# Cross attention in a fused decoder: value products in other pieces, the square turn in two instructions, and TensorE's order in a tile

## What is computed

```python
kv_rope = kv_c * cos[None] + _rotate_half(kv_c) * sin[None]
q_r = jnp.einsum('bshq,hqr->bhsr', q_big, W_qr)
k_r = jnp.einsum('bld,hdr->bhlr', kv_rope, W_kr)
scores = jnp.einsum('bhsr,bhlr->bhsl', q_r, k_r)
attn = jax.nn.softmax(scores, axis=-1)
ctx_c = jnp.einsum('bhsl,bld->bhsd', attn, kv_rope)
ctx_lat = jnp.einsum('bhsd,hkd->bshk', ctx_c, w_kc_kv)
out = ctx_lat.reshape(b, s, H * K) @ Wo.T
```

## Time and profile before

| | |
|---|---|
| time, median of 3 runs | 3219.04 us (3218.99 to 3221.29) |
| profiled execution, its own time | 3230.32 us |
| its span | 3228.3 us |
| granted TensorE clock, mean | 0.952 |
| busy, TensorE | 2933.8 us (91%) |
| busy, VectorE | 1862.5 us (58%) |
| busy, ScalarE | 1242.3 us (38%) |
| busy, POOL | 872.7 us (27%) |

### The profile page before, as it was taken

One profiled execution on the slowest core, in us unless ns is written; L12 is line 12 of the kernel. 1 busy time (PEld: TensorE's weight loads), 2 busy tenths in 40 slices (PEclk: granted clock), 3 DMA queues, 4 the chain that ended last, 5 costly groups with the idle time before them and its releaser, 6 DMA issues. The chain is left out here.

```text
span 3228.3 us, 47818 instructions
## 1 busy us (share of the span) xinstructions
PE 2933.8 (91%) x17993; PEld 1709.2 (53%) x17997; DVE 1862.5 (58%) x3321; ACT 1242.3 (38%) x1997; POOL 872.7 (27%) x743
## 2 busy tenths in 40 slices
PE   4889998988999989899998989989899998677999
PEld 3655555554455453355555557753355555446444
DVE  6557887733232257788885233347788885655222
ACT  3446656521111142455554122222455653424221
POOL 4324555410316024433333000004333333201000
PEclk8899999988999989999999999999999999888999
DMA  1146677622122212277776010012277775001111
GB/s 32 48 120 161 166 174 166 145 66 95 63 91 78 88 28 81 62 165 158 158 165 162 13 42 25 25 43 74 65 170 155 166 168 125 15 12 23 39 39 33
DMA packets 221440, 299.21 MB, mean 93 GB/s; under 512 B 127178, under 2 KB 149052, under 8 KB 218764
## 3 DMA queue, kind: packets, MB, share of 16 engines
q1 hardware_dynamic: 220348, 294.39, 37.4%
q10 hardware_dynamic: 864, 1.77, 0.2%
HBM read 120.52 MB, written 21.38 MB: 44 GB/s over the span
## 5 line engine op out<-in xcount | busy, mean ns | idle before, releaser
L1786 ACT ACTIVATE l1x_shared<-l1x_shared,l1x_a_low 128x1500 f32<-128x1500 f32 x112 | 173.1, 1546 | 159.8 <-DVE l1x_shared L1740 156.9
L1786 ACT ACTIVATE l2x_shared<-l2x_shared,l2x_a_low 128x1500 f32<-128x1500 f32 x112 | 173.1, 1546 | 158.4 <-DVE l2x_shared L1740 156.8
L1786 ACT ACTIVATE l0x_shared<-l0x_shared,l0x_a_low 128x1500 f32<-128x1500 f32 x112 | 173.2, 1546 | 139.5 <-DVE l0x_shared L1740 138.1
L1656 PE MATMUL l0x_a_S_ps<-l0x_kt,l0x_a_q 64*128 64x366 f32 (+1 forms) x896 | 176.4, 507 | 4.4 <-issue 2.5
L1656 PE MATMUL l1x_a_S_ps<-l1x_kt,l1x_a_q 64*128 64x366 f32 (+1 forms) x896 | 175.9, 506 | 2.2 <-DVE l1x_shared L1740 1.9
L1656 PE MATMUL l2x_a_S_ps<-l2x_kt,l2x_a_q 64*128 64x366 f32 (+1 forms) x896 | 174.9, 505 | 2.0 <-DVE l2x_shared L1740 1.6
L2026 DVE TENSOR_TENSOR l0f_times_up<-l0f_gate,l0f_U 128x448 f32<-128x448 f32 x64 | 39.7, 621 | 236.9 <-PE l0f_U L1944 236.9
L1995 ACT ACTIVATE l0f_gate<-l0f_G 128x448 f32<-128x448 f32 x72 | 39.1, 543 | 310.7 <-PE l0f_G L1939 310.7
L1353 POOL TENSOR_TENSOR l2x_q_straight<-l2x_q_straight,l2x_q_crossed 128x448 f32<-128x448 f32 x48 | 54.5, 1135 | 340.5 <-DVE l2x_q_crossed L1344 340.5
L1740 DVE TENSOR_SCALAR_CACHE_REDUCE l0x_shared<-l0x_a_S_ps 128x768 f32<-128x768 f32 x112 | 107.3, 958 | 66.0 <-PE l0x_a_S_ps L1656 57.4
L1740 DVE TENSOR_SCALAR_CACHE_REDUCE l2x_shared<-l2x_a_S_ps 128x768 f32<-128x768 f32 x112 | 107.3, 958 | 53.7 <-PE l2x_a_S_ps L1656 50.2
(11 more groups left out here) (672 smaller groups left out, 6474.2 us busy)
## 6 DMA issues: line engine op xcount, KB each, us to landing
l0x_space<-normed SPq DMA_DIRECT2D x192, 128.0 KB
l1x_space<-normed SPq DMA_DIRECT2D x192, 128.0 KB
l2x_space<-normed SPq DMA_DIRECT2D x192, 128.0 KB
l0x_space<-l0x_a_blocks SPq DMA_DIRECT2D x186, 96.0 KB, 2.8
l1x_space<-l1x_a_blocks SPq DMA_DIRECT2D x186, 96.0 KB, 3.6
...
```

Source lines behind the costliest of these rows:

```text
L1656: last = pe.matmul(S_ps[:, 2 * pair + rows_, 0:w], q[lane, b % 2, k * 128:(k + 1) * 128], kt[lane, b % 2, pair * W1:pair * W1 + w], start= ...
L1786: act.activation(p[:, n % 2], p[:, n % 2], ACT.Exp, bias=low[:, n % 2, 1:2], scale=-1.0, accum_out=den[:, b % 2, k:k + 1]).then_inc(exp_re ...
```

## The change

1. The value products are cut into other pieces: `PIECES` has eight entries in place of seven, with 1, 3, 3, 3, 2 + 1, 4, 4 and 3 slots. The last piece of a batch stands in tile 5 of the next batch (entry 12), where it was in tile 4 (entry 11).
2. TensorE's order in a tile is transposes, values, scores; it was transposes, scores, values.
3. The square turn is two instructions: the six inner squares of each row, then the two outer ones. The first half of `negate`, which overwrites only what the inner squares read, waits for `inner_blocked`, the second half for `outer_blocked`. Whoever waited for `blocked` waits for both.
4. ScalarE copies `C_ps` out one tile later, at tiles 3 and 6.

```diff
--- before.py
+++ after.py
@@ -1430,7 +1430,8 @@
     T, N = QT_TILES, QT_TILES * B
     FIRST, COUNT = (0, 4), (4, 3)
     W1, W2, JB = 3 * KD, KD + 2 * KP, NB * 32
-    PIECES = {5: (0, 0, 2), 6: (0, 2, 4), 7: (0, 4, 8), 8: (0, 8, 12), 9: (1, 0, 4), 10: (1, 4, 8), 11: (1, 8, 12)}
+    PIECES = {5: [(0, 0, 1)], 6: [(0, 1, 4)], 7: [(0, 4, 7)], 8: [(0, 7, 10)], 9: [(0, 10, 12), (1, 0, 1)],
+              10: [(1, 1, 5)], 11: [(1, 5, 9)], 12: [(1, 9, 12)]}
     TURNED_AT = (0, KP, LK - 2 * KP, LK - KP)
     SLOTS = (8, 10, 9, 11, 6, 0, 2, 4, 1, 3, 5, 7)
     ctx, kt, v, nv = ahead.ctx, ahead.kt, ahead.v, ahead.nv
@@ -1467,7 +1468,8 @@
         exp_ready = st.sem(name + "exp_ready")
         turned = st.sem(name + "turned")
         pt_kept = st.sem(name + "pt_kept")
-        blocked = st.sem(name + "blocked")
+        inner_blocked = st.sem(name + "inner_blocked")
+        outer_blocked = st.sem(name + "outer_blocked")
         moved = [[st.sem(f"{name}moved{g}{j}") for j in range(2)] for g in range(2)]
         kept_own = st.sem(name + "kept_own")
         rden_ready = st.sem(name + "rden_ready")
@@ -1493,7 +1495,8 @@
 
         def move(eng, b, g, lanes):
 
-            eng.wait_ge(blocked, T * b + FIRST[g] + COUNT[g])
+            eng.wait_ge(inner_blocked, T * b + FIRST[g] + COUNT[g])
+            eng.wait_ge(outer_blocked, T * b + FIRST[g] + COUNT[g])
             if b > 0:
                 eng.wait_ge(valued, 2 * (b - 1) + g + 1)
             for l in lanes:
@@ -1580,7 +1583,8 @@
 
                 def own(b, g):
 
-                    pool.wait_ge(blocked, T * b + FIRST[g] + COUNT[g])
+                    pool.wait_ge(inner_blocked, T * b + FIRST[g] + COUNT[g])
+                    pool.wait_ge(outer_blocked, T * b + FIRST[g] + COUNT[g])
                     if b > 0:
                         pool.wait_ge(valued, 2 * (b - 1) + g + 1)
                     if ctx is not None:
@@ -1713,16 +1717,17 @@
                 for n in range(N):
                     b, k = n // T, n % T
                     turn(n)
+                    for piece in PIECES.get(k + T, []) if b > 0 else []:
+                        values(b - 1, *piece)
+                    for piece in PIECES.get(k, []):
+                        values(b, *piece)
                     if n + 2 < N:
                         scores(n + 2)
-                    if k > 4:
-                        values(b, *PIECES[k])
-                    elif b > 0:
-                        values(b - 1, *PIECES[k + T])
                     if ctx is not None and k == 4 and b + 1 < B:
                         turn_keys(b + 1)
-                for k in range(T, T + 5):
-                    values(B - 1, *PIECES[k])
+                for k in range(T, T + 6):
+                    for piece in PIECES[k]:
+                        values(B - 1, *piece)
 
             @block.vector
             def _(dve):
@@ -1733,9 +1738,11 @@
                         dve.wait_ge(scored, 2 * n + pair + 1)
                         if pair == 0 and n > 1:
                             dve.wait_ge(turned, n - 1)
-                            dve.wait_ge(blocked, n - 1)
+                            dve.wait_ge(inner_blocked, n - 1)
                         if pair == 1:
                             dve.wait_ge(passed, 2 * n + 1)
+                            if n > 1:
+                                dve.wait_ge(outer_blocked, n - 1)
                         start = n % 2 * LK + at
                         dve.tensor_scalar(ahead.shared[:, start:start + 2 * apart].rearrange("q (a k) -> q a k", a=2)[:, :, 0:w],
                                           S_ps[:, 2 * pair:2 * pair + 2, 0:w],
@@ -1750,8 +1757,10 @@
                     if b > 0 and k == FIRST[g]:
                         dve.wait_ge(moved[g][(b - 1) % 2], 192 * ((b - 1) // 2 + 1))
                         dve.wait_ge(kept_own, 8 * (b - 1) + 4 * g + 4)
-                    dve.transpose(blocks[g][:, :, k - FIRST[g]].rearrange("q l j b -> q j l b"),
-                                  p[:, n % 2, 2 * KP:LK - 2 * KP].rearrange("q (j l b) -> q j l b", j=NB, l=4)).then_inc(blocked, 1)
+                    to = blocks[g][:, :, k - FIRST[g]].rearrange("q l j b -> q j l b")
+                    squares = p[:, n % 2, 2 * KP:LK - 2 * KP].rearrange("q (j l b) -> q j l b", j=NB, l=4)
+                    dve.transpose(to[:, 1:NB - 1], squares[:, 1:NB - 1]).then_inc(inner_blocked, 1)
+                    dve.transpose(to[:, 0:NB:NB - 1], squares[:, 0:NB:NB - 1]).then_inc(outer_blocked, 1)
 
                 def invert(b):
 
@@ -1820,9 +1829,9 @@
                 exp(1)
                 for n in range(N):
                     b, k = n // T, n % T
-                    if k == 2 and b > 0:
+                    if k == 3 and b > 0:
                         keep_contexts(b - 1, 0)
-                    if k == 5 and b > 0:
+                    if k == 6 and b > 0:
                         keep_contexts(b - 1, 1)
                     keep(n)
                     if ctx is not None and k == 4 and b + 1 < B:
```

## The result

The changed kernel takes 3316.37 us (median of 4 runs, 3309.56 to 3323.13), the kernel before 3219.01 us (median of 4, 3214.14 to 3221.29): 1.0304 times as long, with an interval of 1.028 to 1.0329. The profiled execution of the changed kernel took 3309.56 us with a span of 3306.6 us, against 3230.32 and 3228.3: +79.2 us, where the prediction's sum was +79 on that same execution.

What follows compares the result with a forecast made beforehand. The attention loop was taken as bound by TensorE, with a loop through POOL nearly closed in layer 0. Terms 59 + 16 + 4 = +79 us on the profiled 3230.32 gave 3309, put at 3298 us on the median; range 3245 to 3340.

Steps and rivals of the forecast that it cites:

- The offset to the median: Whole kernel: the profiled execution lies 0.35% above the median, so the sum of 3309 us became 3298 us.
- The loop through POOL in layer 0: Last values, POOL's rope and copies, next batch's block products: 32.5 us per batch against 27.97, +59 us.
- the slow clock: Layer 0, after TensorE's wait for POOL: 1.6 us added per batch; +59 us with it, +38 without.
- Which part closes the loop: Layer 0: last values behind the keys' turn and first block product ahead of scores make 30.89 us against 27.97.
- The late moves of layers 1 and 2: Block moves start 1.45 us later and are wanted sooner; nine late batches wait 1.8 us longer, +16 us.
- The split turn: VectorE's square turn: 0.00 to 0.12 us more, a 0.15 us wait given back, hidden behind TensorE; taken as zero.
- Spread pieces and seams: TensorE's tiles: pieces stay 10.15 us, undisturbed batches 24.78 us, seams as before; no gain, seam bound 17 us.
- The ends of the layers: Last tile of the three layers: scores, exponential, turn and moves come one piece later, 3 x 1.45 = +4 us.
- both tight loops snap: Rival, slower still: exponential loop or VectorE's second turn paces most tiles, 34 to 67 us more; chance 0.10.
- the change hardly acts: Rival: POOL's rope was not waiting for the values, layer 0 keeps its period, +4 to +20 us; chance 0.07.
- it is faster: Rival: steadier DMA pace ends late moves of layers 1 and 2, 38 us saved, 3181 us; chance 0.07.

Runs made afterwards that it cites:

- The extra transposes: Changed kernel with 24 unused TensorE transposes per batch laid into its wait for POOL in tile 0 of layer 0: 3312.9 us, 1.0222.
- the inverses in longer runs: Inverse sums laid out in DRAM as (q, k), not (k, q): kernel before 3174.93 us, 0.9853; changed kernel 3258.99 us, 1.0125.
- the copies first: Changed kernel with POOL's own copies of group 0 ahead of its rope: 3259.07 us, 1.0136.

## Why the prediction was right, point by point

3298 us was forecast and 3316.37 measured, within 3245 to 3340, and slower. On the profiled execution the sum was off by less than 1 us, and that is luck: layer 0's loop grew by 75 us (59 forecast), those of layers 1 and 2 by 8 (16 forecast), and the rest shrank by 5 (4 more forecast). The offset to the median missed as well: the changed kernel's median lies 7 us above its profiled execution, where the kernel before lay 11 below.

- **The loop through POOL in layer 0** was the cause, as put: 13 waits of 4.0 us (4.1 forecast), POOL's part 10.20 us (10.18), and the loss goes when the rope stands behind the copies. The term was too small: 33.98 us per batch, not 32.5, +78 us over 13 batches, not +59. What was mis-sized is the slow clock. From last values to last values the loop takes 35.6 us and 32.4 us in turn (one 33.05), where the sum had 31.40 + 1.6 and 30.38 + 1.6. From the first block product of tile 0 to the end of the tile, 2.91 us at full clock, it takes 5.56 us in six long turns of the loop and 4.55 in the six short ones (4.22 in the odd one): 2.1 us lost on average, and not 1.6. In six of the seven batches with the longer keys' turn the last three slots, in tile 5, lose another 1.0 us or more (3.0 us from the transposes' start to their end, and not 1.8), because the clock falls again behind the keys' turn. The sum took the clock as one loss per batch, from a row of layer 1, where there is no keys' turn; with the last values in tile 5 that second fall came to lie within the loop. The two falls together cost 2.6 us per batch where 1.6 was put, and this 1.0 is about two thirds of what the term was short by. Another 0.3 us per batch is a term that the sum left out, for the most part TensorE's wait for ScalarE in front of the keys' turn. The extra transposes bear out the part in tile 0; the one in tile 5 was not taken away by itself.
- **Which part closes the loop** was put partly wrong. The text named two things, the last values behind the keys' turn and the first block product ahead of the scores. The pieces alone give the whole wait (52.7 us) in the old order, and the order alone gives next to none (1.4 us). The order moves both ends of the loop by the same scores, and cancels; only the tile counts. What the order adds in layer 0 is the 0.3 us in front of the keys' turn (that wait is in the run with the order alone, 13 times, and in the run with the pieces alone only once), and some slow clock: 33.98 us per batch against 33.27 with the pieces alone.
- **The late moves of layers 1 and 2** were forecast at +16 us; the loops grew by 8.1 us, and TensorE's waits for moves by 8.2 (24.7 to 32.9). The direction fits, but the term rested on nine late batches being 1.8 us later each, and the moves vary more than that from run to run. With the inverses in longer runs the term is nearly zero. So the margin isn't short by itself: the inverses' transfers eat it.
- **The split turn** was taken as zero, and is, but for batch 0 of layers 1 and 2, which VectorE bounds and which are 1.1 and 1.45 us shorter with the split alone. By their lengths the two turns take 0.13 us more than the one (0.97 and 0.40 us, against 1.24), near the 0.12 us of the forecast's upper end. But each passes VectorE on 0.07 to 0.08 us before its end, so the pair needs 1.22 us; VectorE's tile fell to 3.18 us, below the 3.24 to 3.36 forecast. The Trainium skill (VectorE: DVE Perf Modes, the section on the TRN2 errata) has the extra latency fall between instructions, once for each. The lengths fit that; the starts don't show it, as the second turn starts 0.90 us after a first that lasts 0.97. How long a single turn keeps VectorE when nothing waits for it is in no run.
- **Spread pieces and seams** cost and gain nothing: undisturbed batches 24.75 to 24.77 us in both. What the pieces do is to cover the new order, which with the old pieces costs 0.50 us per batch.
- **The ends of the layers** (+4 us) can't be seen. Outside the loops the changed kernel is 5 us shorter.
- **The rivals:** that both tight loops snap fell, since no undisturbed tile grew; that the change hardly acts, and that it is faster, fell with the 13 waits.

Open stays why the clock falls again in tile 5 behind the same 1.64 us. Of the seven batches from batch 2 on that have this wait it falls in six of the changed kernel, in four with the extra transposes, in three with the order alone, in two with the pieces alone, in one with the copies first, and in none of the kernel before but one of it with the longer runs. So the second fall isn't bound to the changed kernel, and no run shows what decides. Open is also whether it is the store or the fetch of the inverses that holds up the moves.
